# Two attention layers on one core: outputs transposed first in a group's first step, and GpSimd multiplies by the reciprocal sums

## What is computed

```python
x = _L0_xattn_ref(x, ctx_768, ...)            # 8 heads of 40: "main" and "ca"
h1 = _ln(x, n1_g, n1_b)
x = _attn(h1, h1, q1, k1, v1, o1_w, o1_b, 20) + x        # "self", 512 keys
h2 = _ln(x, n2_g, n2_b)
x = _attn(h2, context, q2, k2, v2, o2_w, o2_b, 20) + x   # "cross", 1024 keys
h3 = _ln(x, n3_g, n3_b)
a, g = split(h3 @ ff_w1 + ff_b1, 2)
return a * gelu(g) @ ff_w2 + ff_b2 + x
# _attn: softmax(q k^T * dh**-0.5) v for each head, then @ wo + bo
```

## Time and profile before

| what | value |
|---|---|
| median of three runs | 961.96 us (955.62, 961.96, 968.9) |
| the profiled execution | 959.91 us, of which the span is 958.1 us |
| granted TensorE clock over the span | 0.916 of full speed |
| busy over the span | PE 861.1 us (90%), DVE 624.0 (65%), ACT 470.4 (49%), POOL 65.6 (7%) |
| chain of work that ended last, by engine | PE 60%, DVE 25%, DMA 6%, ACT 4% |
| stream "first" | about 128 to 289 us of the span |
| stream "self" | about 390 to 516 us |
| stream "cross" | about 587 to 812 us (its maxima begin at 560) |

### The profile page before, as it was taken

The page is one execution under the profiler, slowest core; times in us unless marked ns, Lnnn a source line. Parts: engine busy times, 40 slices in busy tenths (PEclk is TensorE's granted clock), DMA queues, the critical chain, the costliest instruction groups (busy, mean ns, idle before and its releaser), DMA issues.

```text
span 958.1 us, 11352 instructions
## 1 busy us (share of the span) xinstructions
PE 861.1 (90%) x4148; PEld 470.2 (49%) x4148; DVE 624.0 (65%) x1178; ACT 470.4 (49%) x682; POOL 65.6 (7%) x87
## 2 busy tenths in 40 slices
PE   4669989999989999989988789999999998789998
PEld 3656744444456675333333544333333332468988
DVE  4244647777673637788774678999999981657141
ACT  4423444445542541555556503766766768456031
POOL 2200001300004021000000300000000000030000
PEclk9877999999997996788789865999999999879999
DMA  6938667532310073122107140222222000500000
GB/s 218 272 106 236 212 183 236 160 101 65 106 42 22 21 247 117 44 66 60 43 1 133 47 129 1 51 52 51 51 51 51 2 1 2 233 1 1 28 1 28
DMA packets 30966, 83.18 MB, mean 87 GB/s; under 512 B 5172, under 2 KB 9212, under 8 KB 28606
## 3 DMA queue, kind: packets, MB, share of 16 engines
q1 hardware_dynamic: 30110, 79.71, 29.2%
q0 software_dynamic: 800, 2.73, 1.0%
HBM read 56.12 MB, written 25.89 MB: 86 GB/s over the span
## 4 chain that ended last, share of the span: by engine, by line
PE 60%; DVE 25%; DMA 6%; ACT 4%; issue 3%; POOL 1%; SPq 1%; DVEq 0%; ACTq 0%; POOLq 0%
PE PS L858 17%; PE PS L801 12%; DVE maxp L960 11%; PE PS L1366 8%; PE PS L553 8%; PE PS L838 6%; DVE negm L960 4%; PE PS L1378 4%; PE PS L1190 3%; DVE turned L990 2%; DMA k_d<-split 2%; DMA ca_nat<-in_ca 2%; ACT probs L924 1%; DMA w_v<-in_Wv 1%; DVE out_t L1009 1%
## 5 line engine op out<-in xcount | busy, mean ns | idle before, releaser
L924 ACT ACTIVATE probs<-PS 128x1024 f32<-128x1024 f32 (+1 forms) x336 | 311.2, 971 | 166.2 <-PE PS L838 161.4
L960 DVE TENSOR_REDUCE maxp<-PS 128x1 f32<-128x512 f32 x448 | 281.2, 679 | 55.2 <-PE PS L801 54.1
L801 PE MATMUL PS<-k_sl,q_sl 48*128 48x512 f32 (+3 forms) x640 | 267.4, 502 | 21.7 <-DMA q_sl<-q_d 11.0
L801 PEld LDWEIGHTS PS<-k_sl,q_sl 48*128 48x128 f32 (+2 forms) x640 | 122.9, 206 | 203.5 <-DVE maxp L960 120.5
L838 PE MATMUL PS<-q_sl,k_sl 50*128 50x512 f32 (+3 forms) x672 | 208.1, 443 | 8.4 <-ACT probs L924 5.2
L960 DVE TENSOR_REDUCE negm<-PS 128x1 f32<-128x512 f32 (+1 forms) x192 | 122.5, 678 | 44.4 <-PE PS L801 43.9
L838 PEld LDWEIGHTS PS<-q_sl,k_sl 50*128 50x128 f32 (+2 forms) x672 | 104.3, 196 | 56.1 <-ACT probs L924 23.8
L858 PE MATMUL PS<-probs,v2c 128*32 128x512 f32 x640 | 86.6, 610 | 5.8 <-DVE turned L990 5.8
L591 DVE TENSOR_TENSOR split<-PS,split 128x512 fp32r<-128x512 f32 (+3 forms) x54 | 34.7, 650 | 49.2 <-ACT split L568 49.1
L858 PE MATMUL PS<-probs,v0c 128*64 128x512 f32 (+1 forms) x256 | 62.9, 612 | 1.5 <-DVE turned L990 0.7
L858 PE MATMUL PS<-probs,v1c 128*32 128x512 f32 x320 | 51.0, 709 | 9.7 <-DVE turned L990 9.7
(11 more groups left out here) (178 smaller groups left out, 979.6 us busy)
## 6 DMA issues: line engine op xcount, KB each, us to landing
k_d<-split SPq DMA_DIRECT2D x20, 512.0 KB, 3.4
q_d<-split SPq DMA_DIRECT2D x12, 512.0 KB, 3.1
k_sl<-k_d SPq DMA_DIRECT2D x8, 640.0 KB
k_sl<-k_d SPq DMA_DIRECT2D x40, 128.0 KB
q_sl<-q_d SPq DMA_DIRECT2D x40, 128.0 KB
k_sl<-k_d SPq DMA_DIRECT2D x20, 256.0 KB
w_raw<-in_ff_w SPq DMA_DIRECT2D x1, 3840.0 KB, 11.8
k_d<-split SPq DMA_DIRECT2D x10, 256.0 KB, 3.7
```

Source lines behind the costliest of these rows:

```text
L801: nc.tensor.matmul(PS[0:a.qt, SBANKS[k % 3], 0:cn], q_view(g)[f:f + a.rows, j // a.stack, q * a.qt:(q + 1) * a.qt], k_view(g)[f:f + a.rows ...
L924: nc.scalar.activation(probs[0:a.size[t], x % PRING, :, 0:a.nq], PS[0:a.size[t], 2 * (x % 2):2 * (x % 2) + 2, 0:a.nq], ACT.Exp, scale=a.sc ...
L960: nc.vector.tensor_reduce((maxp if nch > 1 else negm)[0:a.qt, g.turn, o:o + 1], PS[0:a.qt, SBANKS[k % 3], 0:a.chunks[c][1]], AX.X, ALU.max ...
```

## The change

In a stream, part 0 of `normalise` (the transpose of the finished group's outputs out of PSUM) comes ahead of everything else that DVE does in the first step of a group: ahead of `part_maxima`, where one is due in that step, and of the first reduction. It stood behind the first reduction before. This holds for all three streams. The other parts stay behind the first reduction of their steps.

For stack 2 (self and cross) part 2 leaves DVE. A new function `pool_scale` makes the same product on POOL, one instruction of 128 x 256 elements for each of the 20 groups, in the order of the groups. It waits for the reciprocals (`norm`, now one count a group) and, as before, for `packed` to be free. Its end is signalled on a new semaphore, `scaled`, for which part 3 and the next group's part 0 wait. In POOL's program the products of self stand before the bias additions of the second join, and those of cross behind them.

```diff
         def maxima(chunks, normalising=None):
 
+            if normalising is not None and normalising[1] == 0:
+                normalise(*normalising)
+                normalising = None
             for c in chunks:
                 ended, items = st.chunk(c)
...
                 if i > 0 and a.stack == 2:
-                    dve.wait_ge(st.norm, 2 * i)
+                    dve.wait_ge(st.scaled, i)
                 nc.vector.transpose(turned[:, 0:a.nq], PS[:, OBANK, 0:a.nq]).then_inc(st.out_read, 1)
             elif part == 1:
                 dve.wait_ge(st.out_read, i + 2)
                 nc.vector.reciprocal(recip[:, 0:n], view[:, :, 0]).then_inc(st.norm, 1)
-            elif part == 2:
-                dve.wait_ge(st.norm, 2 * i + 1)
+            elif part == 2 and a.stack == 1:
+                dve.wait_ge(st.norm, i + 1)
                 share_of = recip[:, 0:n].rearrange("p (b o) -> p b o", o=1)
-                if a.stack == 1:
-                    nc.vector.tensor_tensor(view, view, share_of.to_broadcast([128, n, 32]),
-                                            ALU.mult).then_inc(st.norm, 1)
-                else:
-                    if a.tile(g.n) > 0:
-                        dve.wait_ge(a.out_done, a.tile(g.n))
-                    f = D1 * (g.n % (a.groups // B) % 2)
-                    nc.vector.tensor_tensor(packed[:, :].rearrange("p (b r) -> p b r", r=32)[:, :, f:f + D1],
-                                            view[:, :, 1:1 + D1], share_of.to_broadcast([128, n, D1]),
-                                            ALU.mult).then_inc(st.norm, 1)
+                nc.vector.tensor_tensor(view, view, share_of.to_broadcast([128, n, 32]),
+                                        ALU.mult).then_inc(st.scaled, 1)
             elif part == 3 and a.ends_tile(g.n):
-                dve.wait_ge(st.norm, 2 * i + 2)
+                dve.wait_ge(st.scaled, i + 1)
                 nc.vector.transpose(a.dest[:, a.tile(g.n), 0:a.nq], turned[:, 0:a.nq] if a.stack == 1 else packed[:, :]
                                     ).then_inc(a.out_done, 1)
...
+    def pool_scale(pool, st):
+
+        for i, g in enumerate(st.groups):
+            a = g.a
+            n = a.nq // 32
+            pool.wait_ge(st.norm, i + 1)
+            if a.tile(g.n) > 0:
+                pool.wait_ge(a.out_done, a.tile(g.n))
+            f = D1 * (g.n % (a.groups // B) % 2)
+            nc.gpsimd.tensor_tensor(packed[:, :].rearrange("p (b r) -> p b r", r=32)[:, :, f:f + D1],
+                                    turned[:, 0:a.nq].rearrange("p (b r) -> p b r", r=32)[:, :, 1:1 + D1],
+                                    recip[:, 0:n].rearrange("p (b o) -> p b o", o=1).to_broadcast([128, n, D1]),
+                                    ALU.mult).then_inc(st.scaled, 1)
...
+            pool_scale(pool, S_SELF)
             pool.wait_ge(join1.normed, join1.end)
             pool_bias(pool, join2)
+            pool_scale(pool, S_CROSS)
```

More of the change, by code:

```diff
@@ L627, in build @@
         st.norm = sem(f"{n}_norm")
+        st.scaled = sem(f"{n}_scaled")
     q_loaded = [sem(f"q_loaded{s}") for s in range(2 * SLOTS)]
```

## The result

The changed kernel takes 935.39 us (median of six runs, 930.57 to 942.85), the kernel before 963.0 in six runs beside them: a ratio of 0.972, with a 95% interval from 0.965 to 0.979. Forecast were 936.5 against 961.96. The profiled execution of the changed kernel was a quick one, of 930.57 us with a span of 928.8, so its total must not be set against the median; single stages can be compared.

What follows compares the result with a forecast made beforehand. PE was taken as the bound, idle once a group waiting for the transpose, with clock lost in self. -17.4 - 5.5 - 3.5 + 1.0 = -25.4 from 959.91 gives 934.5 profiled, hence a median of 936.5; range 928 to 952.

Steps and rivals of the forecast that it cites:

- Which wait counts: PE's wait for the output transpose, once a group in self, cross and first, together 19.6 us of idle PE.
- Self, -17.4: Transpose ahead in self: gap from 1.14 to about 0.2, clock stays up, groups of 11.7 us; 17.4 us saved.
- the lower bound of -7.4: Least gain in self: 0.93 us saved at each of eight waits, with the clock unchanged.
- rival A: Clock in self goes on falling, so self gives only 7.4 to 10 us; 944 to 947 us, chance 0.2.
- Cross, -5.5: Transpose ahead in cross: gap from 0.72 to about 0.1, gain 0.69 us a group; 5.5 us saved.
- First, -3.5: Transpose ahead in first: gaps of 0.64 us in ca close nearly whole; 3.5 us saved, bounds 0 and -5.
- The product on POOL, 0.85: Product on POOL takes 0.85 us, bounds 0.7 and 1.87, hidden within the streams and not slowing DVE.
- the ends, +1.0: Behind the last group of self and of cross the slower product and crossings cost +0.5 us each.
- The sum: All terms together give -25.4 us, so 934.5 us profiled and a median of 936.5.
- B: DVE becomes the bound and items wait for banks; self groups take 12.2 us, cross gains nothing; 946.5 us, chance 0.1.
- C: Nothing to be seen: PE's wait moves, clock unchanged, gains of 1 to 5 us; 957 to 962 us, chance 0.06.
- D: Slower: the clock falls in cross as DVE holds PE back in one later lump; 982 us, chance 0.04.

Runs made afterwards that it cites:

- run with a gap of 0.55: Changed kernel, but in self the transpose comes behind the two parts of the maxima, ahead of the first reduction; 938.32 us, ratio 0.978.
- table of the gap in four sizes: Kernels with self's transpose at different places: PE gaps of 0.1, 0.55, 1.14 and 1.75 us; seven groups of self took 82.6, 83.5, 98.3 and 114.0 us.

## Why the prediction was right, and where it was not

**Which wait counts.** Right. The transpose alone gives the whole gain.

**Self, -17.4.** Right in size: 15.8 us for the seven groups where 16.4 was forecast, a period of 11.8 where 11.7 was. The clock stayed up, as argued from cross. But the split of this term was worse than its sum. The prediction took the clean group of the earlier trace rows, 12.2 us, for all seven, though it is one without part 3; such groups take 12.29 before and 11.63 now, and those with part 3 take 0.3 more (11.92 now). By an estimate from these rows the seven groups before would have taken 3 x 12.29 + 4 x 12.59 = 87.2 us at full clock and not 85.4. So the lost clock was 11.1 us and not 12.9, and the shorter gap gave the other 4.7 of the 15.8. Closing the gap gave 0.66 a group at full clock, where the lower bound of -7.4, "eight times 0.93, clock as now", and with it rival A's time, had 0.93. The run with a gap of 0.55 shows where the difference lies: the first 0.45 us of gap cost 0.13. Why they are nearly covered was not traced.

**Cross, -5.5.** The mechanism was right, the size a little high: 3.7 us for seven groups where 0.69 each makes 4.8. The step that failed is "the product that leaves DVE (0.42 a group) pays for some of that". It paid 0.2 us in seven groups. A high busy share of DVE over the stage was taken as a sign that its work counts anywhere; it counts in some steps and not in others. The clock of 0.98 that the prediction used for cross belongs to a stretch that begins ahead of its first transpose; from there on its seven groups had 1.00.

**First, -3.5.** From its first to its last transpose the stream takes 280.43 - 139.42 = 141.0 us, before 287.30 - 143.13 = 144.2: -3.2, right.

**The product on POOL, 0.85, and the ends, +1.0.** Both too dear. The product took 0.63 us, less even than the 0.70 that the addition gives in proportion to its elements; which of size, blocks and broadcast does this was not tested. The ends cost +0.25 each, of which 0.21 is the longer product. The 0.1 for the crossings stood on no row, and what is left for them is 0.04. That POOL slows no reduction out of PSUM held with four times the work: four of them took 2.48 us beside the products, as elsewhere. The Trainium skill, "SBUF — State Buffer", section "Who interferes with whom", has VectorE contend with GpSimd in two-port modes or with two SBUF inputs, and never in reductions. By that rule these reductions are free, and the trace agrees. The Trainium skill, "GPSIMD Engine Reference", section "Engine selection", has GpSimd about twice as slow with two inputs, which gives an estimate of 0.84 for the product. Measured were 0.63, 1.5 times VectorE's 0.42, and the measurement decides.

**The sum.** The medians fell by 27.6 us where 25.4 were forecast, and that this is so near is in part luck. Cross was put about 1 us too high and the ends 0.5 too dear, which cancels in part, and by the medians self gave 20 and not 17.4. The two profiles differ by 29.3 us, of which 3.7 lie ahead of the first transpose of first (139.42 against 143.13), where both kernels do the same work.

**The rivals.** A falls by the clock of 1.00. B had DVE as the next bound; it did not take back the gain, though the maxima's parts show that 0.3 us a group are DVE's. C and D did not occur. The Trainium skill, "TensorE: Matmul & The Clock Gate", has in its section on psum-queue depth-cycling that short waits between groups of matmuls make the clock swing. The table of the gap in four sizes agrees: 0.69 to 0.84 at gaps of 1.14 to 1.75 us. The advice in its section "Why this matters for your kernels" is against longer gaps than any of these. By the table these short ones lose clock too, and the measurement decides.

## What to carry to other kernels

Where a stage repeats a short wait of TensorE and its granted clock is under 1.00, count the lost clock beside the wait; here it was over twice what the shorter wait gave by itself. Compare groups of the same work at full clock and at less to get both parts, and see first that they are of one kind on every engine. Before an operation is moved off a full engine, look in which step that engine has idle time: the one that stood there was free here, however full the engine was on average.

## What was not expected of the hardware

In self the cost of a regular gap had a knee between 0.55 and 1.14 us. With the same matmuls in each group, gaps of 0.55 us left the clock at 1.00, gaps of 1.14 brought it to between 0.84 and 0.78, and gaps of 1.75 to 0.69, at 11.9, 14.0 to 14.7, and 16.3 us a group. At 1.14 single groups still went through at 1.00, nearly all of them without part 3. Gaps of 0.72 in cross cost no clock. And GpSimd's product of two inputs in blocks of 16, one of them broadcast, took 0.63 us for 256 elements, against 0.88 for 320 in plain rows.
